# Grouped output matmuls, a weight split moved into attention, and a merge moved to VectorE in a cross-attention and mixture-of-experts kernel

## The reference

```
q = ln @ Wq.T;  kv = concat([xn @ Wkv.T, ln @ Wlkv.T])
attn = softmax(where(mask, (rms(q) * SCALE) @ rms(k).T, -max))
x = x + (attn @ v) @ Wo.T + bo
```

```
probs = softmax(x3 @ router_w.T); weights, indices = top_k(probs, 2)
y = (silu(x3 @ w13_gate[e]) * (x3 @ w13_up[e])) @ w2[e]
x = x + sum over the two experts of weight * y        # x3 = layernorm(x)
```

## Time and profile before

| | us |
|---|---|
| median of three runs (1182.6 to 1185.38) | 1184.58 |
| the profiled execution | 1183.16 |
| its span | 1181.3 |
| PE busy | 1000.8 (85%) |
| POOL busy | 698.9 (59%) |
| VectorE busy | 646.5 (55%) |
| ACT busy | 462.8 (39%) |

### The profile page before, as it was taken

The page is one execution under the profiler, slowest core; times in us unless marked ns, Lnnn a source line. Parts: engine busy times, 40 slices in busy tenths (PEclk is TensorE's granted clock), DMA queues, the critical chain, the costliest instruction groups (busy, mean ns, idle before and its releaser), DMA issues.

```text
span 1181.3 us, 14830 instructions
## 1 busy us (share of the span) xinstructions
PE 1000.8 (85%) x4556; PEld 624.0 (53%) x4557; DVE 646.5 (55%) x1263; ACT 462.8 (39%) x667; POOL 698.9 (59%) x472
## 2 busy tenths in 40 slices
PE   2798506999999999999999999999972169999994
PEld 1565303454555555555555555555442158888884
DVE  3899607655555565555655556555128914444442
ACT  1455501444344544544544554454435013223331
POOL 4024440867787687677668767768756215565553
PEclk9899856999999999999999999999975559999998
DMA  6015550000000000000000000000063064333332
GB/s 184 1 47 185 186 187 22 1 1 1 1 1 1 14 14 1 14 14 2 13 14 5 10 14 14 1 14 14 5 240 143 0 260 124 51 51 50 53 53 27
DMA packets 38206, 59.95 MB, mean 51 GB/s; under 512 B 6827, under 2 KB 26220, under 8 KB 37132
## 3 DMA queue, kind: packets, MB, share of 16 engines
q1 hardware_dynamic: 24270, 42.40, 10.1%
q0 software_dynamic: 7488, 10.23, 5.4%
q10 hardware_dynamic: 6398, 6.69, 1.7%
HBM read 37.29 MB, written 22.02 MB: 50 GB/s over the span
## 4 chain that ended last, share of the span: by engine, by line
PE 73%; DVE 10%; DMA 9%; POOL 2%; issue 2%; ACTq 1%; ACT 1%; SPq 0%; DVEq 0%; POOLq 0%
PE bPV L1255 19%; PE bM L1175 12%; PE bS L1244 9%; PE bS L1245 9%; DMA wsp_d<-wraw 3%; DMA wraw<-w 3%; DVE mpart L877 2%; PE bG L1333 2%; PE bH L1350 1%; PE bY L1333 1%; PE bY L1335 1%; PE bY L1334 1%; PE bT L1190 1%; PE bG L1335 1%; PE bG L1334 1%
## 5 line engine op out<-in xcount | busy, mean ns | idle before, releaser
L877 DVE TENSOR_REDUCE mpart<-bM 128x1 f32<-128x464 f32 x492 | 305.0, 638 | 214.7 <-PE bM L1175 214.4
L441 POOL TENSOR_TENSOR acc_p<-acc_p,PT 128x1024 f32<-128x1024 f32 x160 | 381.2, 2382 | 66.8 <-ACT PT L656 60.5
L656 ACT ACTIVATE PT<-bS 128x1024 f32<-128x1024 f32 (+1 forms) x240 | 237.6, 997 | 321.3 <-PE bS L1245 319.4
L1255 PE MATMUL bPV<-PT,V 128*64 128x512 f32 x928 | 255.0, 617 | 0.0
L1175 PE MATMUL bM<-S,Q 128*128 128x464 f32 x492 | 198.3, 431 | 50.8 <-ACT Q L607 44.8
L1175 PEld LDWEIGHTS bM<-S,Q 128*128 128x128 f32 x492 | 93.4, 190 | 215.6 <-DVE mpart L877 151.3
L1244 PE MATMUL bS<-Q,S 128*128 128x512 f32 x464 | 186.7, 402 | 0.9 <-ACT Q L615 0.7
L1245 PE MATMUL bS<-Q,S 128*128 128x512 f32 x464 | 183.5, 395 | 0.0
L1244 PEld LDWEIGHTS bS<-Q,S 128*128 128x128 f32 x464 | 88.0, 190 | 34.6 <-issue 19.5
L1245 PEld LDWEIGHTS bS<-Q,S 128*128 128x128 f32 x464 | 87.7, 189 | 14.6
L447 POOL TENSOR_TENSOR acc_d<-acc_d,acc_p 128x1024 f32<-128x1024 f32 x16 | 38.0, 2373 | 87.3 <-DVE acc_d L909 87.3
(11 more groups left out here) (223 smaller groups left out, 1533.5 us busy)
## 6 DMA issues: line engine op xcount, KB each, us to landing
W<-wsp_d SPq DMA_DIRECT2D x8, 1536.0 KB, 8.2
wraw<-w SPq DMA_DIRECT2D x24, 256.0 KB, 2.9
wsp_d<-whi SPq DMA_DIRECT2D x24, 256.0 KB, 2.8
wsp_d<-wraw SPq DMA_DIRECT2D x24, 256.0 KB, 3.2
W<-w ACTq DMA_DIRECT2D x4, 1024.0 KB, 10.0
V<-x SPq DMA_DIRECT2D x1, 2048.0 KB, 12.8
W<-w ACTq DMA_DIRECT2D x4, 512.0 KB, 10.9
x<-x SPq DMA_DIRECT2D x12, 128.0 KB, 2.1
```

The lines of the kernel that those rows point to most:

```text
L441: pool.tensor_tensor(acc_p[:], one, PT[:, q % NPT, :, :], ALU.add).then_inc(sem("z_p"), 1)
L656: act.activation(PT[:, p % NPT, 0:n, :], bS[(w.h + p) % 2][:, 0:n, :], ACT.Exp).then_inc(sem("exp"), 1)
L877: dve.tensor_reduce(mpart[:, i, g:g + 1], banks[k % len(banks)][:, 0:PIECE], AX, ALU.max)\
L1255: last = pe.matmul(bPV[b * D:(b + 1) * D, 0, :], V[:, c, h * D:(h + 1) * D], PT[:, p % NPT, b, :], start=c < 2, stop=c >= NK - 2, skip_gro ...
```

## The change

1. **Outputs in groups.** `outputs` of two pairs follow each other: at odd p > 1, outputs(p-3) and outputs(p-2). The last three pairs come behind the unit's transposes of the maxima. `PIECES` is laid out anew to suit.
2. **Weights split inside attention.** All 8 experts are split (96 chunks of 128x256, six per unit). ACT rounds a chunk (`w_hi`) behind the exponentials of pairs 1, 3, 5, 7, 9 and 11; POOL subtracts (`w_lo`) behind its additions 1, 3, 5, 7, 9 and 9. There is one `whi` buffer, so w_hi(n) waits for w_lo(n-1) and for the store of `whi`. VectorE no longer waits for the split before attention. In stage 3, ACT loads the split weights of experts 0 to 3 from `wsp_d`, and the copies and subtractions there are gone.
3. **Loads and stores of `x2`, `x3`** in attention are issued by ACT and no longer by SP.
4. **Sums.** POOL adds pairs 0 to 10 (10 additions), VectorE pairs 11 to 14 (3 additions), and VectorE merges the two sums at the end of a unit.

```diff
-WC = 512
+WC = 256
 NCH = EW // WC
+SHARE = E * NCH // UNITS
...
-            for n in range((E - EARLY) * NCH):
...
-                pool.tensor_copy(whi[:, n % 2, :], wraw[:, n % 2, :]).then_inc(sem("whi"), 1)
...
+            def w_lo(n):
+                pool.wait_ge(sem("whi"), n + 1)
+                pool.tensor_tensor(wraw[:, n % 2, :].bitcast(F32R), wraw[:, n % 2, :], whi[:].bitcast(F32),
+                                   ALU.subtract).then_inc(sem("wsplit"), 1)
...
                     z_sum(w, n)
+                    for k, at in enumerate(LO_AT):
+                        if n == at:
+                            w_lo(SHARE * w.u + k)
...
+            def w_hi(n):
+                act.wait_ge(sem(f"raw{n % 2}"), 16 * (n // 2) + 16)
+                after(act, sem("wst_h"), 16 * n)
+                after(act, sem("wsplit"), n)
+                act.copy(whi[:], wraw[:, n % 2, :]).then_inc(sem("whi"), 1)
...
+                    if p == 1 and w.fin:
+                        x_load(w.tile)
+                    if p in SPLIT_AT:
+                        w_hi(SHARE * u + SPLIT_AT.index(p))
                     if p == HEADS_AT and w.h % 2 == 0 and not w.first:
                         heads_T(w)
                     if p == SD_AT and w.fin:
...
                         act.copy(x3T[:], bT[:, 0, DIM:2 * DIM]...)
+                        x_store(w.tile)
...
             for e in range(EARLY):
-                act.dma_start(W[:, e, 1, 0:N13]..., w13[e, :, :]...)
-                act.dma_start(W[:, e, 1, N13:EW]..., w2[e, :, :]...)
+                for half in range(2):
+                    act.dma_start(W[:, e, half, :].bitcast(F32), wsp_d[e, half, :, :]).then_inc(sem(f"we{e}"), 16)
...
-            for n in range(EARLY * NSC):
...
-                act.copy(W[:, e, 0, c:c + SC], W[:, e, 1, c:c + SC].bitcast(F32)).then_inc(sem("w_hi"), 1)
...
-            dve.wait_ge(sem("wsplit"), (E - EARLY) * NCH)
-            for j in range(2):
-                dve.wait_ge(sem(f"wst{j}"), (E - EARLY) * NCH // 2 * 32)
...
                 for n in range(ND):
                     z_sum(w, n)
+                z_merge(w)
...
-                    if p >= LAG:
-                        outputs(p - LAG)
+                    if p % 2 and p > 1:
+                        outputs(p - 3)
+                        outputs(p - 2)
                     pieces(p, 1)
...
-                for p in range(NP - LAG, NP):
+                for p in range(NP - 3, NP):
                     outputs(p)
...
-PIECES = ((0, 1), (2, 0)) + ((2, 1),) * 3 + ((1, 1), (2, 1), (1, 1), (2, 1)) + ((1, 1),) * 5 + ((0, 0),)
+PIECES = ((1, 0), (2, 0)) + ((1, 0), (2, 2)) * 5 + ((2, 0), (2, 0), (0, 0))
-LAG = 2
-POOL_SUMS = ((0, 1),) + tuple((-1, p) for p in range(2, 12))
-DVE_SUMS = ((12, 13), (-1, 14))
+SPLIT_AT, LO_AT = (1, 3, 5, 7, 9, 11), (1, 3, 5, 7, 9, 9)
+POOL_SUMS = ((0, 1),) + tuple((-1, p) for p in range(2, 11))
+DVE_SUMS = ((11, 12), (-1, 13), (-1, 14))
```

More of the change, by code:

```diff
@@ L133, in build @@
         ident = sb("ident", [P, P])
+        small = ExitStack()
+        mcol = sb("mcol", [P, NK], at=small)
+        cols = sb("cols", [P, 8], at=small)
+        small.close()
+        twin = sb("twin", [P, D], at=small)
+        onec = sb("onec", [P, 1], at=small)
+        mpart = sb("mpart", [P, QB, NG], at=small)
+        cmax = sb("cmax", [P, QB], at=small)
+        orec = sb("orec", [P, QB], at=small)
+        st2 = sb("st2", [P, 6], at=small)
+        mv2 = sb("mv2", [P, 2], at=small)
+        sd2 = sb("sd2", [P, 1], at=small)
+        rs2 = sb("rs2", [P, 1], at=small)
+        small.close()
         wtab = sb("wtab", [P, NBLK])
@@ L200, in build @@
         PT = sb("PT", [P, NPT, 2, QW], at=t1)
[L201 to L205, removed]
         x3T = sb("x3T", [P, 2, P], at=t1)
[L207 to L210, removed]
+        wraw = sb("wraw", [P, 2, WC], at=t1)
+        whi = sb("whi", [P, WC], F32R, at=t1)
         t1.close()
@@ L306, in _ @@
             sp.dma_start(rt[:], router_t.rearrange("(k p) n -> p k n", p=P)).then_inc(sem("c_rt"), 16)
+            sp.wait_ge(sem("klo"), NK)
+            sp.wait_ge(sem("s1"), NK)
+            sp.wait_ge(sem("qT"), NT)
             N13 = (DIM // P) * 2 * I // WC
             def load(n):
-                e, ch = EARLY + n // NCH, n % NCH
-                dst = wraw[:, n % 2, :]
+                e, ch = n // NCH, n % NCH
                 if ch < N13:
@@ L381, in _ @@
                 load_w(e)
-            sp.wait_ge(sem("w_in"), NSC * EARLY)
-            for e in range(EARLY, E):
+            for e in range(E):
                 sp.wait_ge(sem(f"we{e}"), 32)
-                sp.sem_inc(sem("w_in"), NSC)
+                sp.sem_inc(sem("w_in"), 1)
         @block.gpsimd
@@ L695, in _ @@
             act.activation(ra[:], rb[:], ACT.Exp).then_inc(sem("r_ex"), 1)
-            for n in range(EARLY * NSC):
-                e, c = n // NSC, n % NSC * SC
-                act.wait_ge(sem(f"raw_e{e}"), 32)
-                act.copy(W[:, e, 0, c:c + SC], W[:, e, 1, c:c + SC].bitcast(F32)).then_inc(sem("w_hi"), 1)
             def ffn(s, x_, g, h):
@@ L933, in unit @@
                         stats2(t, x2[:], bT[:, 0, 0:DIM], st2[:], mv2[:])
-                    if p == SD_AT + 1 and w.fin:
+                    if p == X3_AT and w.fin:
                         after(dve, sem("ol"), 16 * t)
```

87 lines of the change are left out of this document (33 added, 54 removed).

## The result

The changed kernel took 1139.86 us (median of four runs, 1138.79 to 1141.2), the kernel before 1184.98 beside it: a ratio of 0.9623 (95%: 0.9605 to 0.9641), 45 us less. The forecast was 1122, with 1094 to 1145 as its range. The profiled execution took 1141.2 us with a span of 1139.2.

What follows compares the result with a forecast made beforehand. It took loads, POOL's steps and stores to bound the stretch ahead of attention, PE attention, and VectorE's chain what follows. Terms of -46.8, +12.7 and -28.8 sum to -62.9 us, giving 1122 us, range 1094 to 1145.

Steps and rivals of the forecast that it cites:

- The step that failed: Behind attention: the last tiles' loads, behind 12.6 MB of weights, stay hidden up to double their 6.8 us; no cost.
- the doubled load delays the last tiles: Rival, behind attention: `x2t` waits for most of 12.6 MB, 31 us, 18 behind need; time 1140, chance 0.07.
- a few us: Last tiles behind attention: the delay if DMA engines take turns between queues by packet, leaving the sum as it is.
- Start: Ahead of attention: 40.0 us of waiting go, and 5.8 us by which the split delays VectorE's L795 (between 3 and 6).
- Unit 0: the clock: Start of attention: a 4 us pause, not 44, may let PE score at the higher clock; 1 us saved (0 to 2).
- Grouping: Outputs in attention: 7 groups per unit where there were 14, at 0.36 us each, gain PE 2.5 us per unit.
- The `fin` units: Attention units 4 to 14: POOL and ACT's chain up to `x3T` makes each 43.9 us against 42.4, +16.8 for eleven.
- unit 15: Last attention unit: the same POOL and ACT chain makes it 41.5 us where it took 35.6, +5.9.
- Sums and merge: Unit ends in attention: VectorE's extra sum (1.22 us) and merge (1.9 us) are hidden by PE's last three outputs.
- Issues and PE's clock behind attention: Behind the outputs: ACT's load-issue stall goes, -4.0 us (0 if not); PE may keep its clock, -2 (0 to -4).
- Routing: Behind attention: with POOL idle, twelve VectorE operations fall from 26.0 us to 3.2, -22.8.
- The likeliest case: POOL and ACT's chain sets the `fin` units in attention; time 1108 to 1138, chance 0.66.

Runs made afterwards that it cites:

- half_loads: Changed kernel with ACT's eight loads of experts 0 to 3 issued as sixteen of half the size; 1136.2 us, ratio 0.958 to the kernel before.
- x_first: Changed kernel with ACT's eight loads of experts 0 to 3 issued only after its last copies and the four landed tiles; 1123.25 us, ratio 0.9472.
- best1: Changed kernel with the edits of x_first and sd_first together, one `whi` buffer; 1103.5 us, ratio 0.9299 to the kernel before.
- best2: Changed kernel with the edits of x_first, two_whi and sd_first together; 1100.66 us, ratio 0.9275 to the kernel before.
- best3: best1, with POOL holding back its sum of pair 9 in `fin` units until VectorE's normalisation is done; 1089.44 us, ratio 0.9178.
- two_whi: Changed kernel with two `whi` buffers, so w_hi(n) no longer waits for w_lo(n-1); 1120.63 us, ratio 0.9457 to the kernel before.
- sd_first: Changed kernel with ACT's w_hi placed behind the square root and `x3T`'s copy with its stores; 1115.64 us, ratio 0.9409 to the kernel before.
- pool_busy: Changed kernel with twelve subtractions on an unused buffer added on POOL beside the routing; 1155.27 us, ratio 0.9746 to the kernel before.
- merge_pool: Changed kernel with the merge of the two sums back on POOL; 1140.3 us, ratio 0.9609 to the kernel before.
- group_only: Kernel before with only the change's order of outputs and new `PIECES`; 1159.12 us, ratio 0.9777 to the kernel before.
- fill: best3 with one piece moved ahead of scores(3), where PE waits for exponential 1; 1084.55 us, ratio 0.9158 to the kernel before.

## Why the prediction was right, and where it was wrong

**The step that failed** is "`x2t` behind 6.3 MB landed in 6.8 us and is needed some 13 us behind the outputs: hidden up to double". It cost 14.3 us (+8.3 where -6.0 was forecast). I took the delay as proportional to the bytes outstanding, and hidden by slack. It goes by the length of the other queue's rows. While tiles land, the two queues are served row for row, in the kernel before, in the changed one and in half_loads (288 packets beside 289 in the changed one). ACT's rows went from 1 and 4 KB to 12 KB, and a tile from 0.7 us to 4.04. x_first shows that this is all of the loss. The rival "the doubled load delays the last tiles" had the place and the sign right, at a chance of 0.07, and the size 4 us too large (18), since it let the tiles wait for most of the bytes. That its time, 1140, is the measured one is luck: the start, unit 0 and the grouping make up the difference. The quoted rule of the Trainium skill ("DMA: Bandwidth & Descriptors", section on queues, rings and completion order), that an engine takes turns between queues by packet, agrees with the runs. My reading of it, "a few us", was wrong: I had set no size for a turn, and in bytes it grew with the rows.

**Start: -45.8 forecast, -43.6 measured.** The 40.0 us of waiting went whole. Of the 5.8 us by which the split delayed L795, 3.6 were on the path in the profiled execution; I took all of it and named 3 to 6 as the bounds. The twelve kernels that share this opening cleared `Q2` between 134.86 and 136.73, the changed kernel last, so the term is 3.6 to 5.5.

**Unit 0: the clock.** I took 1 us for scores at the higher clock. It did not come: the first scores take 0.43 us in both kernels, where at full clock they take 0.23. Between the clear and the scores stand 32 maxima of VectorE in 17.5 us, for which PE computes the products. PE's granted clock takes the same course there in both kernels (0.67 in the mean of 137 to 157, and of 181 to 201 before): it rises to 1.00 for some 7 us, is back at 0.50 from 150.5 (before: from 194.5), and stands there when the scores begin at 160.47 (before: 204.08). Idling 4 us ahead of it or 44 makes no difference. The chain of the changed kernel:

```profile
161.69 0.43 PE bS L1238
...
169.57 2.62 PE bPV L1249 x8
172.19 1.07 PE bM L1169 x2
```

The first group of outputs is slow for another reason: 2.62 us where the others take 1.87, and 1.07 where two pieces take 0.62, 1.2 us in all. The clock had risen to 1.00 at 163.7, PE then waited 2.13 us for a maximum, and from 170.5 to 173.5 the granted clock was 0.50 again. best1, best2 and best3 show the same, with a wait of 2.1 us, and take 65.4 to 65.5 us from the clear to the end of unit 0. In x_first, two_whi, sd_first, half_loads, pool_busy and merge_pool, with the same work there, that wait is 1.2 to 1.6 us, the clock stays up, and it is 64.1 to 64.2. There unit 0 gains 1.7 or 1.8, as the grouping gives elsewhere, so 1.2 of the 3.0 us missing in this row are a matter of the execution.

**Grouping: 2.5 forecast per unit, 1.9 measured in units 1 to 3, and 1.6 in units 4 to 14 of group_only.** The term was mis-sized. Two things are missing in it. The group that ends ahead of the transposes of the maxima saves no exit, since these cost 0.44 us instead of 0.53 behind it (0.09 and not 0.20). And there are no outputs left among the first pairs, so that PE waits for exponential 1; the restart takes 0.51 us where a score takes 0.23. fill took that wait away and earned less than half of it, so the second is shown in part only. The chain at the start of unit 1:

```profile
243.29 1.03 ACT PT L644
...
244.37 0.51 PE bS L1238
244.87 0.24 PE bS L1239
```

**The `fin` units: 43.9 forecast, 43.74 measured; unit 15: 41.5 and 41.3.** Right by its own steps: the chain above has the links in the order named, and sd_first shows that the order on ACT carries the cost. Two of its terms were off against each other: `x3T` is done at 440.36 - 404.98 = 35.4 and not at 35.85, and PE's work behind it takes 448.77 - 440.36 = 8.4 and not 7.95. What I did not see is that the chain hides a second one. Where POOL is on time its sum falls on VectorE's normalisation. The prediction names that very pair of instructions, but priced it at a unit's end and not here. It also took the normalisation for a case of two inputs; it has one wide input (`x`) and two columns, and is held up all the same.

**Sums and merge: nothing forecast, nothing measured** (merge_pool, 0.4 us apart, within the intervals).

**Issues and PE's clock behind attention: -4.0 and -2.0 forecast.** The last copy came 1.7 us behind the outputs and not 5.65, but in the changed kernel this saved no time, because the tiles came later still. half_loads, with twice the issues and twice the rows, brought the stall back; it does not tell which of the two counts. PE did not keep its clock: it fell to 0.50 at 843.0, 3 us behind the outputs, and in x_first at 841.8. In x_first the row is 17.1 us, 7.5 less than before where 6.0 were forecast; what gave the part beyond the 4.0 of the issues is not shown.

**Routing: -22.8 forecast, -22.5 measured.** The rule of the Trainium skill's "SBUF — State Buffer" ("SBUF: two separate sides"), that a VectorE instruction with two SBUF inputs and one of GpSimd exclude each other for their whole length, agrees with pool_busy (1.94 beside 1.97 us). best3 shows a like exclusion for the normalisation, which has one wide input: 0.43 us with POOL's sum out of its way, 1.63 in best1.

**The range.** It held the time by 5 us. The likeliest case had been given 1108 to 1138, and 1139.86 lies 2 us beyond that. It was right in its mechanism for attention, and the loss came from a step that had stood in the sum at nothing. The range was wide for the sake of the chain in the `fin` units; that it also covered a miss at the last tiles was not foreseen.

## What to carry to other kernels

A transfer that someone waits for goes ahead of bulk loads in time, on whatever queue: beside them each of its rows waited for about one row of theirs, so that long rows in a bulk load make a short transfer dear, and cutting the rows shorter trades that for the issuing engine's time. Work that nothing on the critical engine needs belongs behind the instructions that it does need, in every in-order stream that it passes; here the place of one copy was 1.8 us in each of eleven units. And where two engines share a port, removing a delay can bring their instructions together: look at the durations in the changed trace and not only at the waits.

## What the runs showed of the hardware

- Transfers of 128 rows of 1 KB landed 4.0 us apart beside another queue's rows of 12 KB, 2.2 us apart beside rows of 6 KB, 0.7 us apart beside rows of 1 KB (two queues, row for row in each case), and 2.0 to 2.2 us behind their issue with the other queue empty.
- ACT's queue took 8 loads of 128 rows (12 KB each) in 4.2 us, and 16 of 6 KB rows in 15 us, during which ACT did nothing else. Of 8 loads with rows of 1 and 4 KB (3072 rows) one issue took 4.0 us.
- VectorE's `tensor_scalar` of 128x256 took 0.41 us alone and 1.60 in the mean beside POOL's sums, without any wait in the trace: such a collision shows in the duration alone. Reductions kept their 0.29 us beside POOL.
- TensorE's granted clock fell from 1.00 to 0.50 in the middle of the first outputs in four executions, where PE had waited 2.1 us just before, and stayed at 1.00 in six with the same work, where it had waited 1.2 to 1.6 us.
- POOL's subtraction of 128x1024 took 1.97 us with the same operand twice and 2.36 with two different ones.
